# Last-layer attention in six-unit cycles, its maxima taken from rounded factors by two row halves of TensorE at once

## The reference, cut to what matters

```python
def _L3_conv_ref(...):                      # layer 3; x is (2, 48, 48, 192), 12 heads of 16
    qkv = imagelike_bhwc @ qkv_w + qkv_b
    ...
    q, k, v = (qkv[0], qkv[1], qkv[2])
    attn = jnp.einsum('bqd,bkd->bqk', q * scale, k)
    ...
    rel_h = jnp.einsum('bhwc,hkc->bhwk', r_q, Rh)
    rel_w = jnp.einsum('bhwc,wkc->bhwk', r_q, Rw)
    bias = (rel_h[:, :, :, :, None] + rel_w[:, :, :, None, :]).reshape(b * nh, n, n)
    attn = jax.nn.softmax(attn + bias, axis=-1)
    out = jnp.einsum('bqk,bkd->bqd', attn, v)
    ...
    return out @ proj_w + proj_b
...
    x = x + _L0_conv_ref(_gn(x), ...)          # windowed attention
    x = x + _L1_conv_ref(_gn(x), ...)          # two layers of a selective scan
    x = x + _L2_conv_ref(_gn(x), ...)
    x = x + _L3_conv_ref(_gn(x), ...)
    return x
```

## Time and profile before

| | us |
|---|---|
| median of 3 runs (lowest to highest) | 5249.56 (5249.46 to 5252.27) |
| the profiled execution, its own time | 5256.67 |
| its span, first to last instruction | 5254.9 |

### The profile page before, as it was taken

The page is one execution under the profiler, slowest core; times in us unless marked ns, Lnnn a source line. Parts: engine busy times, 40 slices in busy tenths (PEclk is TensorE's granted clock), DMA queues, the critical chain, the costliest instruction groups (busy, mean ns, idle before and its releaser), DMA issues. The chain is left out here.

```text
span 5254.9 us, 74962 instructions
## 1 busy us (share of the span) xinstructions
PE 3881.1 (74%) x22962; PEld 1489.1 (28%) x22962; DVE 3805.5 (72%) x5393; ACT 2674.3 (51%) x3467; POOL 1469.1 (28%) x941
## 2 busy tenths in 40 slices
PE   5588784531778774623877766759999999999997
PEld 3244442210122221210222213342333333333332
DVE  4355553586999993586999974458787787887784
ACT  1255452384555542583555542244666666666663
POOL 0000000001999990003999970000000000000000
PEclk9788897765888887755888877858999999999998
DMA  3310104033222212133222220241111111111112
GB/s 104 99 29 20 29 20 77 29 94 113 67 63 64 70 45 57 39 113 96 69 63 62 71 67 22 101 138 42 45 45 45 45 45 45 45 44 39 48 41 68
DMA packets 153460, 317.93 MB, mean 61 GB/s; under 512 B 37811, under 2 KB 96188, under 8 KB 149095
## 3 DMA queue, kind: packets, MB, share of 16 engines
q1 hardware_dynamic: 153062, 312.85, 22.0%
HBM read 204.28 MB, written 108.02 MB: 59 GB/s over the span
## 5 line engine op out<-in xcount | busy, mean ns | idle before, releaser
L1869 DVE TENSOR_REDUCE l3a_mx<-l3a_mx 128x1 f32<-128x384 f32 x2719 | 1325.1, 548 | 349.3 <-PE l3a_mx L1739 340.5
L1844 ACT ACTIVATE l3a_p<-l3a_s 128x1024 f32<-128x1024 f32 (+1 forms) x1080 | 978.2, 936 | 424.1 <-PE l3a_s L1760 418.1
L1252 POOL TENSOR_TENSOR l_scan_sc<-l_scan_s,l_scan_repc 128x768 f32<-128x768 f32 x576 | 1036.2, 1861 | 5.7 <-DVE l_scan_s L1230 5.7
L1739 PE MATMUL l3a_mx<-l3a_k,l3a_q 124*128 124x384 f16 x2719 | 868.4, 340 | 21.1 <-issue 17.3
L1189 ACT ACTIVATE l_scan_da<-l_scan_da,l_scan_a 128x768 f32<-128x768 f32 x576 | 504.0, 875 | 631.7 <-PE l_scan_da L1113 631.5
L1760 PE MATMUL l3a_s<-l3a_q,l3a_k 125*128 125x512 f16 (+1 forms) x2160 | 752.6, 363 | 27.8 <-issue 27.8
L1113 PE MATMUL l_scan_dup<-l_scan_du,l_scan_pick 96*128 96x512 bf16 (+1 forms) x1152 | 348.9, 392 | 368.0 <-DMA l_scan_dt<-l_dtp 212.9
L1778 PE MATMUL l3a_o<-l3a_p,l3a_vh 128*32 128x512 f32 (+1 forms) x4332 | 592.2, 566 | 0.0
L1243 POOL TENSOR_TENSOR l_scan_bup<-l_scan_dus,l_scan_repb 128x768 f32<-128x768 f32 x192 | 357.0, 1859 | 653.4 <-DMA l_scan_repc<-l_bcp 653.4
L1707 POOL TENSOR_TENSOR l3a_norm<-l3a_out,l3a_spread 128x512 f32<-128x512 f32 x25 | 32.2, 1287 | 1622.0 <-DMA l3a_spread<-l_inverses 1622.0
L1739 PEld LDWEIGHTS l3a_mx<-l3a_k,l3a_q 124*128 124x128 f16 x2719 | 265.1, 98 | 711.2 <-DVE l3a_mx L1869 580.9
(11 more groups left out here) (194 smaller groups left out, 4532.8 us busy)
## 6 DMA issues: line engine op xcount, KB each, us to landing
l3a_q<-l_qx SPq DMA_DIRECT2D x104, 486.0 KB
l_scan_du<-l_dup SPq DMA_DIRECT2D x144, 144.0 KB
l_scan_dt<-l_dtp SPq DMA_DIRECT2D x144, 144.0 KB
l_scan_repb<-l_bcp SPq DMA_DIRECT2D x48, 384.0 KB
l_scan_repc<-l_bcp SPq DMA_DIRECT2D x48, 384.0 KB
l3a_q<-l_hx SPq DMA_DIRECT2D x104, 72.0 KB
l_dtp<-l_prep_high_t SPq DMA_DIRECT2D x16, 432.0 KB, 3.2
l_dup<-l_prep_high_u SPq DMA_DIRECT2D x16, 432.0 KB, 3.1
```

The costliest lines, as they stand in the source:

```text
L1252: pool.tensor_tensor(SC[:, st % NSC, :], S[:, n, :], REPC[k % 2][:], ALU.mult).then_inc(weighted, 1)
L1739: pe.matmul(out[:, 0:RG], Q[h % HPB][0:rows, variant(g), qt * 128:(qt + 1) * 128], K[h % HPB][0:rows, g * RG:(g + 1) * RG], start=True, st ...
L1844: act.activation(P[:, g % NP, :, 0:w], s_ps[n % 2][:, :, 0:w], ACT.Exp).then_inc(exped, 1)
L1869: dve.tensor_reduce(MX[:, h % HPB, qt, g:g + 1], mx_ps[bank][:, 0:RG], AX_X, ALU.max)\
```

## The change

In the new order an iteration holds six heads. A unit is one key tile by 384 queries, 108 a head, with three one-bank score buffers. Six units make a cycle: in it PE runs six scores, one maxima pair after units 1, 3 and 5, and after unit 3 the values of two key tiles. The 2304 queries are taken in two halves of 1152. A value product has one key tile's weights in all four column groups and a quarter of the half, 288 queries, in each; the sums of a half stay in o_ps until its 18 key tiles are done. So there is no fold and no copy into OS; ACT copies o_ps out twice a head.

The maxima are found from the rounded factors alone: 16 + 30 + 8 = 54 rows for 124. These are loaded a second time, into QM and KM, at partitions 0 to 53 for the first half of the queries and 64 to 117 for the second (load_tops, 1.1 MB a head). A pair of matmuls, one in each half of the array's rows, writes two banks, and one DVE instruction reduces both. 54 pairs a head take the place of 108 matmuls; mx_ps is a ring of two pairs. The other buffers of Q, K and VH go from three to two. Exponentials are in a ring of six half rows. The load of a query's four variants is one transfer, not four. The sums are stored apart from the output. The parts of the query and key are stored in another order (last lines), so that the rounded ones lie next to the bias.

The diff, cut to its core:

```diff
...
-    HPB = 3
+    HPB = 6
+    NB = 2
     NI = BH // HPB
+    PB = HPB // NB
     KT = L // 128
-    NQC = len(LCH)
-    PAIRS = KT // 2
-    SPH = NQC * PAIRS
-    ST = HPB * SPH
+    NHALF = 2
+    HALF = L // NHALF
+    QG = HALF // 4
+    SW = 384
+    THIRDS = HALF // SW
+    KPH = NHALF * KT
+    UPH = KPH * THIRDS
+    ST = HPB * UPH
+    CYC = 2 * THIRDS
     RG = 8 * W
     NRG = L // RG
     VAR = RK // 8
-    NMX = KT * NRG
-    NR = 3
-    AHEAD, FOLD_AT, JOIN_AT, TURN_AT, INVERT_AT = 8, 6, 2, 6, 20
-    QUADS = [(qc, a, min(2, PAIRS - a)) for qc in range(NQC) for a in range(0, PAIRS, 2)]
-    NQD = len(QUADS)
+    TOP = HD + RW + 8
+    TPH = KT // 2
+    NMX = TPH * NRG
+    NR, NS_PS, NP = 2, 3, 6
+    AHEAD, JOIN_AT, TURN_AT, INVERT_AT = 4 * CYC, 1, 3, 6 * CYC
+    V_AT, OUT_AT, MX_AT = 3, 5, (1, 3, 5)
     ONE = 2 * HD
-    NP = 5
-    LOADS, SHIFTS, STORES = 16 * (2 * VAR + 1), 16 * VAR, 16 * NQC
+    LOADS, TOPS, SHIFTS, STORES = 16 * 3, 16 * 6, 16 * VAR, 16 * 4
...
-        P = s.sb("p", [128, NP, 2, CH])
-        MX = s.sb("mx", [128, HPB, KT, NRG])
+        Q = [s.sb(f"q{i}", [KROWS, VAR, L], F16) for i in range(NB)]
+        K = [s.sb(f"k{i}", [KROWS, L], F16) for i in range(NB)]
+        QM = [s.sb(f"qm{i}", [128, VAR, HALF], F16) for i in range(NB)]
+        KM = [s.sb(f"km{i}", [128, L], F16) for i in range(NB)]
+        VH = [s.sb(f"vh{i}", [128, KT, ONE]) for i in range(NB)]
...
-        s_ps = [s.ps(f"s{i}", [128, 2, CH]) for i in range(2)]
-        mx_ps = [s.ps(f"mx{i}", [128, CH]) for i in range(NR)]
+        SPREAD = s.sb("spread", [128, NHALF, QG])
+        NORM = s.sb("norm", [128, NHALF, QG])
+        s_ps = [s.ps(f"s{i}", [128, CH]) for i in range(NS_PS)]
+        mx_ps = [s.ps(f"mx{i}", [128, 2, CH]) for i in range(NR)]
         o_ps = s.ps("o", [128, CH])
...
+        def values_at(g):
+
+            e, x = divmod(g, UPH)
+            if x % CYC != V_AT:
+                return []
+            back, k = (e, x // CYC * 2 - 2) if x >= CYC else (e - 1, KPH - 2)
+            return [(back, k), (back, k + 1)]
+
+        def half_ends_at(g):
+
+            e, x = divmod(g, UPH)
+            if x % CYC != OUT_AT:
+                return []
+            back, k = (e, x // CYC * 2 - 1) if x >= CYC else (e - 1, KPH - 1)
+            return [(back, k // KT)] if k % KT == KT - 1 else []
 
...
-        def stream(g, place):
-
-            e, x = divmod(g, SPH)
-            ahead, slot = divmod(x + AHEAD, SPH)
-            return [(e + 1 + ahead, pos, what) for pos, what in mx_at.get((slot, place), [])]
+            u = pos - (pos > TURN_AT)
+            mx_at.setdefault(u // len(MX_AT) * CYC + MX_AT[u % len(MX_AT)], []).append((pos, what))
+
+        def stream(g):
+
...
+              .then_inc(loaded[buf], 16)
+
+        def load_tops(sp, head, buf):
+
+            for a in range(2):
+                at, half = 64 * a, slice(a * HALF, (a + 1) * HALF)
+                sp.dma_start(KM[buf][at:at + HD, :], kx_dram[bass.ds(head, 1), 0:HD, :].rearrange("a r l -> (a r) l"))\
+                  .then_inc(tops_loaded[buf], 16)
+                sp.dma_start(QM[buf][at:at + HD + RW, :, :],
+                             qx_dram[bass.ds(head, 1), 2 * HD:3 * HD + RW, half].rearrange("a r l -> (a r) l")
+                             .unsqueeze(1).to_broadcast([HD + RW, VAR, HALF])).then_inc(tops_loaded[buf], 16)
+                sp.dma_start(QM[buf][at + HD + RW:at + TOP, :, :],
+                             hx_dram[bass.ds(head, 1), :, 0, half].rearrange("a (v r) l -> (a r) v l", v=VAR))\
+                  .then_inc(tops_loaded[buf], 16)
...
+        def store_sums(sp, row, buf, count):
+
+            for g in range(4):
+                sp.dma_start(by_group(sum_dram[bass.ds(row, 1), :], g), OUT[32 * g + HD:32 * g + HD + 1, buf, :, :])\
+                  .then_inc(sums_stored, 16)
             sp.wait_ge(sums_stored, count * STORES + LEAD)
             sp.dma_start(SUMS[:], sum_dram[bass.ds(row, 1), :].rearrange("a (p n) -> (a p) n", p=128))\
               .then_inc(sums_loaded, 16)
+
+        def store_out(sp, row, count):
+
             sp.wait_ge(inverted, count + LEAD)
             sp.dma_start(inv_dram[bass.ds(row, 1), :].rearrange("a (p n) -> (a p) n", p=128), INV[:])\
...
+                        sp.wait_ge(mx_taken, i * (HPB * NX) + (e * NX + NX + LEAD))
+                        load_tops(sp, (i * HPB + e + 2) % BH, e % NB)
+                        sp.wait_ge(o_taken, i * (HPB * NHALF) + (e * NHALF + LEAD))
+                        store_sums(sp, i * HPB + e, (e + 1) % 2, i * HPB + (e + 1))
+                        sp.wait_ge(scored, i * ST + (e * UPH + LEAD))
+                        load_head(sp, (i * HPB + e + 1) % BH, (e + 1) % NB)
                         store_out(sp, i * HPB + e, i * HPB + (e + 1))
                         sp.wait_ge(mx_taken, i * (HPB * NX) + ((e + 2) * NX + TURN_AT + 1 + LEAD))
-                        load_shift(sp, (e + 1) % HPB)
-                sp.wait_ge(exped, NI * NU + 1 + LEAD)
+                        load_shift(sp, (e + 1) % NB)
...
                 def mx_pass(number, h, bank, what):
@@ -1732,122 +1756,87 @@
                     pe.wait_ge(mx_taken, number + (LEAD + 1 - NR))
                     out = mx_ps[bank]
                     if what[0] == "turn":
-                        pe.transpose(out[0:KT, 0:128], M[:], eye[:, :]).then_inc(mx_made, 1)
+                        pe.transpose(out[0:KT, 0, 0:128], M[:], eye[:, :]).then_inc(mx_made, 1)
                     else:
-                        qt, g = divmod(what[1], NRG)
-                        rows = KROWS - 1
-                        pe.matmul(out[:, 0:RG], Q[h % HPB][0:rows, variant(g), qt * 128:(qt + 1) * 128],
-                                  K[h % HPB][0:rows, g * RG:(g + 1) * RG], start=True, stop=True)\
-                          .then_inc(mx_made, 1)
-
...
+                def maxima(i, g):
+                    for h, pos, what in stream(g):
                         if pos == 0:
...
+                def score(i, g):
+                    e, x = divmod(g, UPH)
+                    k, third = divmod(x, THIRDS)
+                    half, kt = divmod(k, KT)
+                    at = half * HALF + third * SW
+                    if x == 0:
+                        pe.wait_ge(loaded[e % NB], i * (PB * LOADS) + (e // NB + 1) * LOADS)
+                        pe.wait_ge(shift_loaded[e % NB], i * (PB * SHIFTS) + (e // NB + 1) * SHIFTS)
+                    pe.wait_ge(exped, i * ST + (g + 1 - NS_PS + LEAD))
+                    pe.matmul(s_ps[g % NS_PS][:, 0:SW], K[e % NB][:, kt * 128:(kt + 1) * 128],
+                              Q[e % NB][:, variant(kt * 128 // RG), at:at + SW], start=True, stop=True)\
+                      .then_inc(scored, 1)
+
+                def values(i, e, k):
+                    half, kt = divmod(k, KT)
+                    pe.wait_ge(exped, i * ST + (e * UPH + (k + 1) * THIRDS + LEAD))
+                    if k == 0:
+                        pe.wait_ge(v_ready[e % NB], i * PB + (e // NB + 1))
+                    if kt == 0:
+                        pe.wait_ge(o_taken, i * (HPB * NHALF) + (e * NHALF + half + LEAD))
+                    for g in range(4):
+                        mm = pe.matmul(o_ps[32 * g:32 * g + 32, 0:QG], VH[e % NB][:, kt, :],
+                                       P[:, k % NP, g * QG:(g + 1) * QG], start=kt == 0, stop=kt == KT - 1)
                     mm.then_inc(summed, 1)
...
                 with pe.Fori(0, NI) as i:
                     for g in range(ST):
-                        e, x = divmod(g, SPH)
-                        if x == FOLD_AT:
-                            fold(i, e - 1, unit_of["fold", e - 1])
-                        score(i, g, 0)
-                        maxima(i, g, 0)
-                        score(i, g, 1)
-                        maxima(i, g, 1)
...
+                def take_out(i, e, half):
+                    act.wait_ge(summed, i * (HPB * KPH) + (e * KPH + (half + 1) * KT + LEAD))
+                    act.wait_ge(divided, i * HPB + (e + LEAD))
+                    act.activation(OUT[:, e % 2, half, :], o_ps[:, 0:QG], ACT.Copy).then_inc(o_taken, 1)
 
...
-                for g in range(2):
-                    for f, qc in ends_at.get(g, []):
-                        take_o(NI, f, qc)
-                take_out(NI, -1, 0)
+                        e, x = divmod(g, UPH)
+                        k, third = divmod(x, THIRDS)
+                        act.wait_ge(scored, i * ST + (g + 1 + LEAD))
+                        if third == 0:
+
+                            act.wait_ge(summed, i * (HPB * KPH) + (e * KPH + k - NP + 1 + LEAD))
+                        act.activation(P[:, k % NP, third * SW:(third + 1) * SW], s_ps[g % NS_PS][:, 0:SW], ACT.Exp)\
+                           .then_inc(exped, 1)
+                        for f, half in half_ends_at(g):
+                            take_out(i, f, half)
...
```

(33 more changed lines are left out.)

240 lines of the change are left out of this document (77 added, 163 removed).

## The result

The changed kernel takes 5190.89 us (median of 4 runs, 5185.75 to 5194.19) where the kernel before takes 5249.51 (4 runs, 5245.55 to 5252.27). The ratio is 0.9888, with a 95% interval of 0.9871 to 0.9905: 58.6 us less, 1.1%. Forecast were 94 us less and 5156.

The account below looks back on a forecast made before the run. PE was taken to bound the loop, 62.8 of 64.3 us a head. Loop -60, iteration ends -24 and start -10 gave -94, from the profiled 5256.7 to 5163; the runs' median is 7.1 lower, so 5156; range 5085 to 5300.

Parts of the forecast that it names:

- What bounds the kernel: Last layer's attention loop before the change: PE's own work is 62.8 of 64.3 us a head; coupling adds 2%.
- The loop through ACT: In a six-unit cycle, waits between PE and ACT's exponentials set the length: 3.31 us, taken as 3.35 with coupling.
- PE's sum: PE's own work in a cycle: scores 1.0, maxima 0.95, values 1.21, together 3.16 us.
- The drain between modes: Changing TensorE's tiling mode drains it, seven times a cycle; priced at 0.10 us in and 0.07 out for maxima pairs.
- The row halves run at once: In the loop's maxima, a pair costs what one matmul does, 0.17 us, removing 9.2 us of a head.
- That rival: Maxima pairs run as two matmuls in turn; cycle 3.7 to 3.75 us, 5317 us, slower; chance 0.19.
- free modes: Row mode changes around maxima pairs cost nothing; cycle 3.21 us, 5095 us; chance 0.13.
- exponentials in line: ACT's exponentials don't overlap at this size; cycle 3.51 us, 5224 us; chance 0.12.
- a lower clock: PE's clock falls to 0.88 in the loop; cycle 3.55 us, 5242 us, no change; chance 0.08.
- The iteration's end: Each loop iteration's end costs 6.0 us; 3 ends in the window for 7 save 24 us.
- The start: Before the loop, PE waits for fewer loaded bytes before its first maxima: 10 us saved, between nothing and 17.3.
- the loads inside the loop: SP's queue carries 1.1 MB a head more, 5 us at 226 GB/s, costed at nothing.

Follow-up runs that it names:

- the experiment with two buffers: The changed kernel with two score buffers in place of three; 5414.56 us.
- the run in one half: The changed kernel with both matmuls of a maxima pair in the lower row half (partitions 0 to 53), still into two banks; 5345.56 us.
- the 23-row kernel: The changed kernel with the 46-row transfer of the queries' rounded factors cut into 23 and 23 rows; 5544.06 us.
- with the pair moved: The changed kernel with the middle pair of maxima after unit 2, not after unit 3; 5222.78 us.

## Why the prediction was right, and where it was off

**What bounds the kernel.** That PE bounded the loop before, with prices by starts, held: the same prices gave the new loop's 61.8 us a head for a measured 61.31.

**The loop through ACT.** Right in mechanism and size: 3.31 by the count and 3.35 with the allowance for coupling, for a measured 3.34 us; the idle of 0.9 for 0.93; and the experiment with two buffers moves it, though by more than the same count said (3.95 for 3.70). PE's sum was priced at 3.16 and is 3.21; the way out of a pair is 0.10 (4001.30 to 4001.57 less 0.17), not the 0.07 read in the first layer. The drain between modes that was weighed against the change is real; its price for row halves is 0.20 in and out, between the 0.17 taken and the 0.24 of the column groups.

**The row halves run at once**: right, shown by the pair of 0.34 us and by the run in one half. That rival would have given 5317; it was built and took 5346.

**The rivals** of free modes, exponentials in line and a lower clock fell: the way out of a pair is 0.10; six exponentials take 2.42, which is 5 x 0.386 + 0.49; the clock stays at 0.99.

**The iteration's end.** The step took 6.0 us for each; the three cost 26 us and not 18. The prediction called the end one jump; it left out that PE, with three small score buffers, also waits for ACT to start over (3.51 us at 3994.10). Heads that were 0.5 us shorter than forecast (12 us) hide this and some 4 us more in the window, beyond heads and ends, which weren't followed. That the loop came out at 84.6 for 84 is partly luck, because these cancel.

**The start: wrong, and this is the whole miss.** The step was "10 by the share of bytes", with bounds from 0 to 17.3 less. In its place the way from the first transfer to the first maxima grew by 27.8 us, and the maxima started 22.5 later. The step priced the loads by bytes at the old rate; it didn't ask how many engines a transfer of another shape gets. Its bounds ran from no gain to 17.3 us; a loss was not among them, though nothing in the trace excluded one. The same step put the loads inside the loop at 5 us by the 226 GB/s of the earlier trace rows. At 50 GB/s the two of 46 rows alone (0.85 MB) take 17, and only because the sums' inverses are awaited a third of a head later does that cost nothing; the 23-row kernel, where they take twice as long, shows the price.

The forecast of 5156 was 35 us too low; the start accounts for 36 (+26.1 for -10), the loop for less than one; the 5.3 us ahead of the stage and the difference between profiled runs and medians (63.2 us less against 58.6) cancel.

## What to carry to other kernels

Where a change alters the shape of a transfer, price it by engines times rate, not by bytes: take the largest divisor of its rows up to 16, and compare the DMA share of the old rows with that. A gain in TensorE's columns through tiles must be set against every change of mode around it, 0.10 us on each side here: grouping work of one mode beside another that needs the change anyway is what makes it pay. Where a value group shuts a consumer out, count the loop from its last buffer back to itself by starts. It told the changed kernel's cycle within 0.03 us (3.31 for 3.34), which busy shares (ACT 71%, PE 97% of the loop) don't tell; for the variants with two buffers and with the pair moved it was 0.25 and 0.11 to 0.15 too short, since each brought waits that the count had left out. With small buffers, ask too what an engine's late restart at an iteration's end costs the others.

## What the runs showed of the hardware

A transfer of 46 rows of 2304 bytes ran at 50 GB/s and one of 23 such rows at 25 (share 0.06 of 16 engines); with 16 and 30 rows all engines were busy, but moved 141 to 148 GB/s in all. Two f16 matmuls of 54 rows and 384 columns in the two row halves took the time of one (0.333 us each, both within 0.34), and in one half 0.16 us more. Between a matmul over the whole array and one in a row half lie 0.10 us in each direction beyond the stream. An iteration's end cost 8.2 to 9.5 us with six heads in the body, 9.5 with twelve (17.9 us for two ends fewer), and 5.4 to 7.0 with three. At an iteration's start ACT loaded a table for 1.28 us in both kernels.
